# Deep experts of a four-layer MetaFormer: norming with tokens on partitions between transposes, one product for the gates, and the last stage's two norms moved into its loop

## Reference

```python
t = t + ffn(_ln_t(t))                      # _ln_t: (v - mean) / sqrt(var + 1e-5) over the 64 channels
# ffn, L0 and L2: the router and the experts read the same normed x
w = top-2 softmax of (x @ Wg + bg), as 8 dense weights a token
out = sum_e w[:, e] * (gelu(x @ W1[e] + b1[e]) @ W2[e] + b2[e])
# ffn, L3: the router reads the normed x, and the experts norm it a second time
logits = xt @ Wr + br
xn = (xt - mean(xt)) * rsqrt(var(xt) + 1e-5)
```

## Time and the profile before

| what | value |
|---|---|
| median of 3 runs | 1927.13 us (1922.31 to 1930.56) |
| span of the profiled execution | 1914.4 us |
| its own device time | not given apart; the runs lie 7.9 to 16.2 us above the span, their median 12.7 |
| instructions | 51089 |
| PE busy | 1705.4 us, 89% |
| DVE, ACT, POOL busy | 915.8, 912.6, 521.6 us |
| L0 stage, from its start-up to its last tile's end | 137.4 to 416.2 us |
| `layer_norm_twice` | 1622.0 to 1654.6 us |
| L3 stage | 1654.7 to 1914.4 us |

### The profile page before, as it was taken

The page is one execution under the profiler, slowest core; times in us unless marked ns, Lnnn a source line. Parts: engine busy times, 40 slices in busy tenths (PEclk is TensorE's granted clock), DMA queues, the critical chain, the costliest instruction groups (busy, mean ns, idle before and its releaser), DMA issues. The chain is left out here.

```text
span 1914.4 us, 51089 instructions
## 1 busy us (share of the span) xinstructions
PE 1705.4 (89%) x21120; PEld 788.8 (41%) x21120; DVE 915.8 (48%) x1920; ACT 912.6 (48%) x1210; POOL 521.6 (27%) x692
## 2 busy tenths in 40 slices
PE   7989999998998899789888877999999587699998
PEld 3543444433333333233777762444443232233333
DVE  3544444534665556430566654444543277243433
ACT  3225555554555344444444436355555500655554
POOL 0001222220000254501566652022222055032223
PEclk8999999998999899899899988999999898799999
DMA  5003223220000566057234411223232030134242
GB/s 241 12 11 71 64 46 89 45 45 34 12 1 23 132 147 144 18 202 289 77 100 133 138 42 69 45 56 79 45 89 46 5 37 3 41 93 112 73 112 61
DMA packets 64242, 147.46 MB, mean 77 GB/s; under 512 B 35512, under 2 KB 35640, under 8 KB 59920
## 3 DMA queue, kind: packets, MB, share of 16 engines
q1 hardware_dynamic: 64144, 146.22, 28.4%
HBM read 106.07 MB, written 25.44 MB: 69 GB/s over the span
## 5 line engine op out<-in xcount | busy, mean ns | idle before, releaser
L1295 ACT ACTIVATE ARENA<-PS,W 128x1024 f32<-128x1024 f32 x384 | 406.6, 1111 | 248.3 <-PE PS L1228 164.8
L1127 POOL TENSOR_TENSOR ARENA<-ARENA 128x512 f32<-128x512 f32 x168 | 214.2, 1275 | 786.7 <-DVE ARENA L1417 786.1
L1200 PE MATMUL PS<-ARENA,W 64*128 64x512 f32 x1536 | 358.3, 606 | 3.4 <-DVE ARENA L1348 3.4
L1228 PE MATMUL PS<-ARENA,W 128*64 128x512 f32 x1536 | 350.8, 599 | 2.6 <-DVE ARENA L1417 2.6
L1417 DVE SCALAR_TENSOR_TENSOR ARENA<-PS,W,ARENA 128x512 f32<-128x512 f32 x192 | 143.3, 750 | 325.7 <-PE PS L1228 304.8
L1200 PEld LDWEIGHTS PS<-ARENA,W 64*128 64x128 f32 x1536 | 141.0, 187 | 205.4 <-issue 104.5
L1228 PEld LDWEIGHTS PS<-ARENA,W 128*64 128x64 f32 x1536 | 101.8, 136 | 214.6 <-issue 206.5
L635 POOL TENSOR_TENSOR ARENA<-ARENA 128x512 f32<-128x512 f32 x56 | 71.0, 1268 | 296.3 <-DVE ARENA L969 294.7
L2346 PE MATMUL PS<-ARENA 32*32 32x32 f32 x8448 | 103.2, 197 | 5.7 <-issue 5.4
L807 ACT ACTIVATE ARENA<-PS,W 128x1024 f32<-128x1024 f32 x64 | 67.9, 1111 | 68.8 <-PE PS L711 68.8
L2346 PEld LDWEIGHTS PS<-ARENA 32*32 32x32 f32 x8448 | 93.4, 106 | 8.6 <-issue 6.1
(11 more groups left out here) (249 smaller groups left out, 2352.6 us busy)
## 6 DMA issues: line engine op xcount, KB each, us to landing
ARENA<-scratch_g SPq DMA_DIRECT2D x64, 768.0 KB, 9.6
ARENA<-scratch_g SPq DMA_DIRECT2D x64, 256.0 KB, 3.9
W<-w_dram SPq DMA_DIRECT2D x1, 7307.5 KB, 25.1
ARENA<-XN SPq DMA_DIRECT2D x12, 512.0 KB, 3.8
ARENA<-XN SPq DMA_DIRECT2D x24, 256.0 KB, 2.5
scratch_x<-ARENA SPq DMA_DIRECT2D x8, 512.0 KB, 3.9
scratch_b<-ARENA SPq DMA_DIRECT2D x8, 512.0 KB, 4.1
scratch_z<-ARENA SPq DMA_DIRECT2D x8, 512.0 KB, 3.9
```

The lines of the kernel that those rows point to most:

```text
L1127: nc.gpsimd.tensor_tensor(SUM[:, k, :], SUM[:, k, :], TMP[:, e % 2, :], ALU.add)\
L1200: last = mm(PS[:, (u % UPS) * R + r, :], w(layer + "_w1", b * 128, (b + 1) * 128, half(r)), XS[half(r), t % 2, :], start=True, stop=True)
L1228: last = mm(PS[half(r), out_of(e), :], w(layer + "_w2", b * C, (b + 1) * C), H[:, u % HS, r * T:(r + 1) * T], start=part == 0, stop=part = ...
L1295: f(H[:, u % HS, :], PS[:, at:at + R, :].rearrange("p a b -> p (a b)"), ACT.Gelu, bias=w(layer + "_b1", b, b + 1)).then_inc(e_gelu.sem, 1)
```

## The change

The centred, normed tile is made with tokens on partitions. Four transposes turn the tile of X (`turn_in`); DVE sums over the 64 channels and subtracts the mean in one pass each (`center`); ACT squares; DVE sums the squares, takes the inverse root and multiplies the turned tile by it (`invert`); four transposes turn it back (`turn_back`); ACT copies it to XS (`copy`), and the logits are made from XS. The centre, mean-of-squares and scale products go. The gates of all four groups are turned by one product of 128 columns (GATE as 64 weight columns), and the layout of the gates in DRAM and WB changes to fit: each spread DMA now has four runs a partition of a quarter of the length. The bytes stay.

L3 uses the same loop with `renorm=True`: two inverse roots are taken at once, the experts use the one of the double norm, and the logits are multiplied by RATIO to give those of the single norm. `layer_norm_twice` and the input DMAs of that stage are gone.

The steps' places change: `in` at n = 0, `back` at n = 1, the logits behind the downs of n = 1; `square` (0, 3), `copy` (1, 3), `bend` (2, 3), `rows` (3, 2) on ACT; `invert` behind the scaling of e0 on DVE. In the start-up two fill products stand behind each step but the last.

```diff
-        def layer_norm_twice(once, twice, src):
-            a = Arena()
-            FLY = 4
-            SQ, LOG, INV, LOG2, INV2 = (a.take(FLY, T) for _ in range(5))
...
-            WB, TMP, SUM = a.take(2, E, T), a.take(2, T), a.take(2, T)
+            WB, TMP, SUM = a.take(2, G, E * TOK), a.take(2, T), a.take(2, T)
...
+            gates = gate_dram[sorted(HIDDEN).index(layer)].rearrange("n r e t -> n (r e t)")\
+                .rearrange("n (g r x) -> n g r x", g=G, r=R)
+            SQ, CEN = a.take(T), a.take(T)
+            KINDS = 2 if renorm else 1
+            TOTAL, RATIO = a.take(GR), a.take(GR)
+            VAR, INV, NEWT = (a.take(KINDS * GR) for _ in range(3))
+            EXPERT_INV = INV[:, (KINDS - 1) * GR:]
             L, M, SC, S1, S2, GATE = (a.take(GR, E) for _ in range(6))
             M1, M2, W1, W2 = (a.take(GR) for _ in range(4))
             D = a.take(GR)
-            GATES = GATE.rearrange("p (g r) e -> p g (r e)", r=R)
-            NEWTON = 2 + 3 * 3
-            RANK, WEIGH = 11 + 1 + norms, 3 + 2
-            VARIED = slice(GR * E, GR * E + GR)
+            NEWTON = 2 + KINDS + 2 + 3 * 3 + 2 * (KINDS - 1)
+            RANK, WEIGH = 11 + KINDS, 3 + 2
...
-            if norms:
-                order = ["center", 0, 1, "logits", 2, 3, "scale", 4, 5, "turn", 6, 7]
-                after_scale = {0: 0, 2: 2, 4: 4, 6: 6, "center": -1, "logits": 1, "scale": 3, "turn": 5}
-                at_last = {3: 1, 5: 3, 7: 5}
-                pe_at = {0: "center", 0.5: "logits", 2: "scale", 3: "turn"}
-                act_at = {(0, 1): "square", (1, 1): "widen", (2, 1): "bend", (3, 1): "rows"}
-                dve_at = {-1: "keep", 1: "invert", 3: "rank norm", 4: "weigh"}
-            else:
-                order = [0, 1, "logits", 2, 3, 4, 5, "turn", 6, 7]
-                after_scale = {0: -1, 1: 0, 2: 2, 4: 3, 5: 4, 6: 6, "logits": 1, "turn": 5}
-                at_last = {7: 5}
-                pe_at = {1: "logits", 3: "turn"}
-                act_at = {(1, 3): "bend", (3, 1): "rows"}
-                dve_at = {1: "rank", 3: "weigh"}
+            order = ["in", 0, 1, "back", 2, 3, "logits", 4, 5, "turn", 6, 7]
+            after_scale = {0: 0, 2: 2, 4: 4, 6: 6, "in": -1, "back": 1, "logits": 3, "turn": 5}
+            at_last = {3: 1, 5: 3, 7: 5}
+            pe_at = {0: "in", 1: "back", 1.5: "logits", 3: "turn"}
+            act_at = {(0, 3): "square", (1, 3): "copy", (2, 3): "bend", (3, 2): "rows"}
+            dve_at = {-1: "center", 0: "invert", 3: "rank", 4: "weigh"}
...
                     def spread(p):
                         k = p % 2
                         sp.wait_ge(g_rows.sem, g_rows.at(p + 1))
-                        sp.dma_start(gates[p].rearrange("r e t -> (r e) t"), RT[0:GW, k, :])\
+                        sp.dma_start(gates[p].rearrange("g r (e t) -> (g r e) t", e=E), RT[0:G * GW, k, 0:TOK])\
                             .then_inc(g_kept.sem, 16)
                         sp.wait_ge(g_kept.sem, g_kept.at((p + 1) * 16))
                         if p > 1:
@@ -1083,30 +1022,18 @@
                             sp.wait_ge(e_scaled.sem, e_scaled.at((p - 1) * E))
                         for lo, hi, done in ((0, EARLY, e_first[k]), (EARLY, E, e_rest[k])):
                             for r in range(R):
-                                sp.dma_start(WB[half(r), k, lo:hi, :],
-                                             gates[p, r:r + 1, lo:hi, :].to_broadcast([C, hi - lo, T]))\
+                                sp.dma_start(WB[half(r), k, :, lo * TOK:hi * TOK],
+                                             gates[p:p + 1, :, r, lo * TOK:hi * TOK]
+                                             .to_broadcast([C, G, (hi - lo) * TOK]))\
                                     .then_inc(done.sem, 16)
...
-                    def center(p):
-                        behind("center", p - 1)
-                        mm(PS[:, out_of("center"), :], w("center"), tile(X, p),
-                           start=True, stop=True).then_inc(ln_centered.sem, 1)
+                    def turn_in(p):
+                        behind("in", p - 1)
+                        for g in range(G):
+                            last = nc.tensor.transpose(PS[:, out_of("in"), g * TOK:(g + 1) * TOK],
+                                                       X[:, p * T + g * TOK:p * T + (g + 1) * TOK], w("ident"))
+                        last.then_inc(ln_centered.sem, 1)
+
+                    def turn_back(p):
+                        behind("back", p - 1)
+                        pe.wait_ge(ln_scaled.sem, ln_scaled.at(p + 1))
+                        for g in range(G):
+                            last = nc.tensor.transpose(PS[:, out_of("back"), g * TOK:(g + 1) * TOK],
+                                                       CEN[:, g * TOK:(g + 1) * TOK], w("ident"))
+                        last.then_inc(ln_varied.sem, 1)
 
                     def logits(p):
                         behind("logits", p - 1)
-                        if norms:
-                            pe.wait_ge(ln_taken.sem, ln_taken.at(p * 2 + 1))
-                        else:
-                            pe.wait_ge(e_input[p % 2].sem, e_input[p % 2].at((p // 2 + 1) * INPUT))
+                        pe.wait_ge(ln_normed.sem, ln_normed.at(p + 1))
                         for g in range(G):
                             last = mm(PS[:, out_of("logits"), g * R * E:(g + 1) * R * E],
-                                      CEN[:, g * TOK:(g + 1) * TOK] if norms else XR[:, p % 2, g * TOK:(g + 1) * TOK],
-                                      w(layer + "_wg"), start=True, stop=True)
+                                      XS[:, p % 2, g * TOK:(g + 1) * TOK], w(layer + "_wg"), start=True, stop=True)
                         last.then_inc(g_logits.sem, 1)
-                        if norms:
-                            pe.wait_ge(ln_squared.sem, ln_squared.at(p + 1))
-                            for g in range(G):
-                                last = mm(PS[:, out_of("logits"), GR * E + g * R:GR * E + (g + 1) * R],
-                                          SQ[:, g * TOK:(g + 1) * TOK], w("mean64")[:, 0:P:C], start=True, stop=True)
-                            last.then_inc(ln_varied.sem, 1)
-
-                    def scale(p):
-                        behind("scale", p - 1)
-                        pe.wait_ge(ln_log.sem, ln_log.at(p + 1))
-                        for g in range(G):
-                            last = mm(PS[:, out_of("scale"), g * TOK:(g + 1) * TOK],
-                                      WIDE[:, g, :], w("ident"), start=True, stop=True)
-                        last.then_inc(ln_scaled.sem, 1)
                     def transpose(p):
                         behind("turn", p - 1)
                         pe.wait_ge(g_split.sem, g_split.at(p + 1))
-                        for g in range(G):
-                            last = mm(PS[0:GW, out_of("turn"), g * TOK:(g + 1) * TOK], GATES[:, g, :], w("ident"),
-                                      start=True, stop=True)
-                        last.then_inc(g_turned.sem, 1)
+                        mm(PS[0:G * GW, out_of("turn"), 0:TOK], GATE.rearrange("p a e -> p (a e)"), w("ident"),
+                           start=True, stop=True).then_inc(g_turned.sem, 1)
...
                     def up(u):
                         t, b = divmod(u, NB)
-                        if norms and b == 0:
+                        if b == 0:
                             pe.wait_ge(ln_normed.sem, ln_normed.at(t + 1))
...
                         elif e == 7:
                             pe.wait_ge(g_rows.sem, g_rows.at(t + 2))
-                        elif norms and e == 1:
-                            pe.wait_ge(ln_taken.sem, ln_taken.at((t + 1) * 2 + 1))
-                        elif norms and e == 5:
+                        elif e == 1:
+                            pe.wait_ge(ln_taken.sem, ln_taken.at(t + 2))
+                        elif e == 3:
                             pe.wait_ge(ln_normed.sem, ln_normed.at(t + 2))
                         else:
                             pe.wait_ge(g_taken.sem, g_taken.at(t + 2))
                         prepare(pe_at[n], 0)
-                        if norms and pe_at[n] != "turn":
-                            fill(UPS * R - 1, 1 + (pe_at[n] == "logits"))
+                        if pe_at[n] != "turn":
+                            fill(UPS * R - 1, 2)
...
                     def square(p):
 
-                        act.wait_ge(ln_taken.sem, ln_taken.at(p * 2 + 1))
+                        act.wait_ge(ln_taken.sem, ln_taken.at(p + 1))
                         f(SQ, CEN, ACT.Square).then_inc(ln_squared.sem, 1)
 
-                    def widen(p):
-
-                        act.wait_ge(ln_newton.sem, ln_newton.at((p + 1) * NEWTON))
-                        f(WIDE.rearrange("p g (r c) -> p (g r) c", r=R), INV.unsqueeze(2).to_broadcast([P, GR, C]),
```

(84 more changed lines are left out.)

104 lines of the change are left out of this document (13 added, 91 removed).

## The result

The changed kernel takes 2037.22 us, median of 4 runs (2032.63 to 2043.97), against 1927.03 before: ratio 1.057, 95% interval 1.054 to 1.060. The difference of the medians is 110.2 us; the sum of the prediction was 81 + 25 = 106. Between the two profiled executions it is 116.0 (spans 2030.4 and 1914.4). The profiled execution of after took 2032.63 us, the lowest of its four.

What follows compares the result with a forecast made beforehand. PE was taken to bound the kernel, its queue full inside the stages. Span 1914.4 + 81 (PE work, waits, start-ups) + 25 (clock) = 2020, or 2033 us with the 12.7 between median and profiled span; range 2000 to 2060.

Steps and rivals of the forecast that it cites:

- PE work: PE's queue, per prepared tile: preparation of 2.4 us instead of 5.0 in L0 and L2 (-2.6); +0.4 in L3.
- Wait 1: PE at `turn_back` waits for `invert`, behind the late square: 1.6 us a tile in L0 and L2, 2.25 in L3.
- Wait 2: PE ahead of expert e3 waits for ScalarE's copy, placed behind gelu 11: 3.0 us in every prepared tile.
- Wait 3: PE ahead of expert e7 waits for the rows copy, placed behind gelu 18: 1.65 us a tile, all stages.
- Tiles: Expected sign: L0 tiles of 37.6 to 39 us instead of 33.9, L3 tiles of 38.2 to 40 instead of 30.85.
- The clock: PE's granted clock falls after idle stretches close together: three tiles in four, 1.6 us each, +25 us (bounds 0 and 36).
- Start-ups: Stage starts: +0.9 us each in L0 and L2; -23.3 in L3, where `layer_norm_twice` goes and the start-up grows.
- DMAs: Gate store and spreads: the early part lands 1.9 us before e0's scaling, so nothing was charged.
- rival (c): Late gates at e0's scaling: shorter runs make the early spread land later, 57 us, 2090 us; chance 0.06.
- Rival (b): The waits do not arise, shown at e3's start; PE's queue alone decides: -55 us, 1872 us; chance 0.05.

Runs made afterwards that it cites:

- e0: Not a run: the first expert of a tile; VectorE's scaling of its output waits for the gates' spread.
- e2: Not a run: an expert of a tile; its downs follow `turn_back` on PE and need a bank freed by an earlier scaling.
- e3: Not a run: an expert of a tile; its downs use the bank of `turn_back` and wait for ScalarE's copy.
- e6: Not a run: an expert of a tile, in the last batch; gelu 18 waits for its output.
- the best version: Changed kernel with square, copy and rows moved earlier, `invert` ahead of the first expert's scaling, start-up fills together, early gate spread of four experts: 1870.25 us, ratio 0.970.
- the last two edits: To the kernel with three steps moved: `invert` ahead of the first expert's scaling and six fills behind `turn_in`, 1884.92 us; then early spread of four experts, 1870.25 us.
- e7: Not a run: an expert of a tile, in the last batch; PE waits ahead of it for ScalarE's rows copy.

## Why the prediction was right, step by step

- **PE work.** Forecast 2.4 us of preparation a tile. The rows give 0.58 + 0.57 + 1.00 + 0.27 = 2.42, and the tile without waits takes 31.25 us, 2.62 under 33.87. Right. The Trainium skill (TensorE: Matmul & The Clock Gate, section PE-mode transpose) has about 275 ns for one bf16 transpose in a kernel; here f32 ones take 147 ns each back to back.
- **Wait 1**, forecast 1.6 us in L0 and L2 and 2.25 in L3: measured 1.41, and in L3 1.70 plus 0.55 ahead of e2 = 2.25. The square ends 4.69 us behind D0 (250.72 - 246.03), forecast 4.8.
- **Wait 2**, forecast 3.0: measured 2.75 in every prepared tile.
- **Wait 3**, forecast 1.65: measured 1.42. The brackets sum to 5.58 us in an L0 tile, but it is 37.33 - 31.25 = 6.08 longer than one without them, as a row of downs that stops and starts again is longer (eight alone take 1.94, sixteen in a row 3.65); forecast 6.25. The three were worked out from where gelus stand behind expert outputs; moving the copy and the rows copy forward by two and one gelus took their waits away in every tile, and with the square moved too none is left in five of the six L0 tiles after the first, so this cause is shown.
- **Tiles.** 37.33 us in L0 (forecast 37.5 without the clock), 38.2 in L3 (30.85 + 7.3 = 38.15).
- **The clock**, forecast +25 as three tiles in four at 1.6 us. Beyond undisturbed tiles the periods of L0 hold 12 us, those of L3 17, and L2 some 4; L3's last prepared tile, which no `turn_in` follows, adds 1.5. Of these 35, about 7 are the first tiles' longer waits. So the clock cost about 28. That this is near 25 is luck: nine tiles were slow (two in L0, one in L2, six in L3) where 16 were forecast, and one cost 3.1 us instead of 1.6. The reason given for the share, that two idle stretches stand close together, is not borne out either: with the square moved, e3's downs were slow in L0 with no stretch ahead of `turn_back`. That the same 2.75 us cost nothing in 259.99 and much in 219.39 was not foreseen, nor that the loss depends on the other waits.
- **Start-ups**, forecast +0.9 each in L0 and L2: from the first row to the first downs it is 22.9 us (136.91 to 159.77) against 20.05, +2.8, near the upper bound. PE idles 4.32 us ahead of `turn_back` and then makes its fills at half clock. L2: 22.55 (1243.49 to 1266.04) against 20.05, +2.5. L3: 23.7 against 47.8 before, -24.1, forecast -23.3. The L0 and L2 terms were thus mis-sized, by 1.9 and 1.6 us.
- **DMAs**, charged at nothing. The early part of the spread lands after 5.5 us (3.9 before), the rest after 10.7 (9.6). The 1.9 us of cover were not there: in every later tile that prepares another e0's scaling waits 0.6 to 2.9 us for the gates, in the steady L0 tile 1.15 (it starts at 248.70, 12.2 behind the start of e6's downs, where the landing was put at 9.5). That costs nothing there only because `invert` has to wait for the square until 250.72 anyway (in the L0 tile where it waits 2.89 us, 0.35 is lost); with the square early and the rows copy late, it came to light. In first tiles it costs time at once: e0's scaling is 4.48 us behind. That part of rival (c) is real, about 2 us a stage.

The first tile of the changed kernel, in its timeline:

```profile
165.77 0.75 DVE L1329 SCALAR_TENSOR_TENSOR ARENA<-PS,W,ARENA 128x512 f32<-128x512 f32 x1 [4.48 <-DMA ARENA<-scratch_g]
...
170.60 1.08 PE L1082 MATMUL PS<-W,ARENA 128*128 128x128 f32 x4 [3.54 <-DVE ARENA L1260]
```

And its issues by line, as the earlier trace rows:

```profile
ARENA<-scratch_g SPq DMA_DIRECT2D x64, 768.0 KB, 10.7
ARENA<-scratch_g SPq DMA_DIRECT2D x64, 256.0 KB, 5.5
```

So the sum was 106 against 110.2 between medians and 116.0 between the two profiles. Of the 10 us to the latter, 3.5 - 0.8 are start-ups, about 7 the first tiles and 3 the clock, and the waits of L0 and L2 were 14 x 0.17 = 2.4 too large; that makes 10. Rival (b), at 1872, was a sound estimate of a steady tile (31.25 us in L0, as it has it). That the best version's 1870.25 meets it is partly luck: moving the three steps alone gave 1890.68, and the last two edits made the start-ups shorter than the rival had them (19.75 us in L0 against 20.05 + 0.9), while L3's tiles stayed above it, at 31.7.

## What to carry over

When a step is moved in a queue written by hand, work out not when its input is ready but when the instruction ahead of it is released: here two gelus that wait for a buffer decided. If removing one of several short waits gives next to nothing, look at the granted clock behind the one that is left, before dropping the theory: the waits, with the clock that hung on them, were worth 146 us together and 83 apart. And read first tiles by themselves; they have less cover than the rest.

## What the runs showed of the hardware

- An idle stretch of 2.75 us is followed by the lower level (1.2 GHz) in some tiles and not in others, with the same work ahead. With the 1.42 us wait ahead of e7 removed, seven L0 tiles of seven were slow in place of two; with the one ahead of `turn_back` removed, six. Less idle time in a tile thus went with more slow tiles, and the earlier trace rows show the lower level behind 3.04 us alone, not behind a stretch this short. The Trainium skill (TensorE: Matmul & The Clock Gate, section Loop structure matters more than you think) says that the loop nest decides whether matmuls keep their rate, in the case of long DMA waits; the runs show it for waits of 2.75 us on ScalarE. What exactly tips a tile stays open.
- Idle products of 2.84 us in the place of a wait that was left in gave 12 us back, and with them two other removals gave 74.7 us in place of 1.7 and 7.6.
- A broadcast of the same bytes in four runs a partition of a quarter of the length landed 1.6 us later in the median (5.5 against 3.9). Other transfers around it changed as well, so the share of the runs' length was not measured by itself.
